# Feed-forward of a decoder layer: order of the inner and down parts, the last inner tile, and the closing sums

## What is computed

```python
gate = x2 @ Wg          # 512 -> 1376
up = x2 @ Wu            # 512 -> 1376
inter = gate * jax.nn.sigmoid(gate) * up
out = (inter @ Wd).astype(jnp.float16)   # 1376 -> 512
```

## Time and profile before

| | us |
|---|---|
| median of 3 runs | 779.55 (778.93 to 779.99) |
| the profiled execution, its time | 780.11 |
| its span in the trace | 777.8 |
| first matmul of window 0 | 632.25 |
| first matmul of window 10 | 741.63 |
| first matmul of the down parts of tile 10 | 761.90 |

### The profile page before, as it was taken

How to read it: one execution, slowest core, us unless ns; L and a number is a source line. 1 busy time by engine, 2 the same in 40 slices (tenths; PEclk the granted TensorE clock), 3 DMA queues, 4 the chain that set the end, 5 groups by cost and what they waited for, 6 DMA issues and landing times.

```text
span 777.8 us, 11268 instructions
## 1 busy us (share of the span) xinstructions
PE 749.0 (96%) x3764; PEld 623.4 (80%) x3764; DVE 504.4 (65%) x664; ACT 383.3 (49%) x964; POOL 308.3 (40%) x333
## 2 busy tenths in 40 slices
PE   7999999999999999999999999999999869999994
PEld 6888888888888888888888888888887647777763
...
GB/s 298 110 56 78 14 91 108 77 69 35 155 30 104 47 128 0 94 108 57 48 37 135 30 65 24 111 0 262 22 1 2 1 0 78 59 81 35 28 10 108
DMA packets 43807, 54.34 MB, mean 70 GB/s; under 512 B 7400, under 2 KB 26024, under 8 KB 43784
## 3 DMA queue, kind: packets, MB, share of 16 engines
...
## 4 chain that ended last, share of the span: by engine, by line
PE 89%; DVE 4%; POOL 2%; issue 2%; ACT 2%; DMA 1%; SPq 0%; DVEq 0%; POOLq 0%; ACTq 0%
PE psum L425 20%; PE psum L427 20%; PE psum L426 20%; PE psum L552 7%; PE psum L626 6%; PE psum L627 5%; PE psum L561 3%; PE psum L634 3%; PE psum L635 2%; PE psum L431 1%; DVE stats L1032 1%; PE psum L445 1%; DMA xacc<-in_x 1%; PE psum L530 1%; DVE xacc L1265 1%
## 5 line engine op out<-in xcount | busy, mean ns | idle before, releaser
L954 POOL TENSOR_TENSOR probs<-probs,rowinv 128x512 f32<-128x512 f32 x64 | 71.1, 1111 | 308.7 <-DVE rowinv L1177 308.7
L785 ACT ACTIVATE probs<-probs,negmax 128x128 f32<-128x128 f32 x256 | 99.8, 391 | 60.4 <-DVE negmax L1164 60.4
L425 PE MATMUL psum<-xt_hi,wq_hi 128*128 128x512 f32 x256 | 104.4, 408 | 0.0
L425 PE MATMUL psum<-wo_hi,at_hi 128*128 128x512 f32 x256 | 100.2, 391 | 0.5 <-DVE at_lo L1195 0.5
L427 PE MATMUL psum<-xt_hi,wq_lo 128*128 128x512 f32 x256 | 100.2, 391 | 0.0
L426 PE MATMUL psum<-xt_lo,wq_hi 128*128 128x512 f32 x256 | 99.9, 390 | 0.0
L427 PE MATMUL psum<-wo_hi,at_lo 128*128 128x512 f32 x256 | 99.7, 389 | 0.0
L426 PE MATMUL psum<-wo_lo,at_hi 128*128 128x512 f32 x256 | 99.6, 389 | 0.0
L778 ACT CAST pt_hi<-psum 128x512 fp32r<-128x512 f32 x64 | 37.5, 587 | 124.6 <-PE psum L561 124.6
L1195 DVE TENSOR_TENSOR at_lo<-psum,at_hi 128x512 fp32r<-128x512 f32 x64 | 44.1, 689 | 72.7 <-ACT at_hi L814 72.7
L689 ACT ACTIVATE qt<-psum 128x512 f32<-128x512 f32 x64 | 38.0, 594 | 75.7 <-PE psum L427 74.1
(11 more groups left out here) (128 smaller groups left out, 1647.0 us busy)
## 6 DMA issues: line engine op xcount, KB each, us to landing
...
```

The lines of the kernel that those rows point to most:

```text
L425: pe.matmul(dst, a_hi, b_hi, start=start, stop=False)
L785: e = act.activation(probs[:, t % 2, j, :], probs[:, t % 2, j, :], ACT.Exp, bias=negmax[:, t % 2, j:j + 1], accum_out=rowsum[:, t % 2, j:j ...
L954: pool.tensor_tensor(probs[:, t % 2], probs[:, t % 2], rowinv[:, t % 2, :].unsqueeze(2).to_broadcast([P, HG, P]), ALU.mult).then_inc(prob_ ...
```

## The change

Four edits. **Order:** in windows 2 to 10 the down parts stand between the gate and up parts: positions 0 to 3 gate and up, 4 down 0, 5 and 6 gate and up, 7 down 2, 8 and 9 gate and up, 10 down 1, 11 down 3. ACT takes positions 0, 1, 4 and 7, DVE the others; on ACT both down parts now stand ahead of Silu, and on POOL the sum of down part 0 ahead of the inner product. **Last inner tile:** the product and int_lo of tile 10 are made by DVE. **Closing sums:** DVE does all four chunks of token half 0 and chunks 2 and 3 of half 1; ACT and POOL do chunks 0 and 1 of half 1. ACT and POOL add output blocks 1, 3 and 6, over y_part. **Tail of the attention:** the first token halves of the first four gate and up parts of window 0 are computed in slots 10 to 13, one in each, into even banks.

```diff
+        GU_AT = (0, 1, 2, 3, 5, 6, 8, 9)
+        D_AT = (4, 10, 7, 11)
+        ACT_AT = (0, 1, 4, 7)
+        LAST_WINDOW = NT + LAG - 2
+
+        def gu_at(n, k):
+            return GU_AT[k] if n >= LAG else k
+
+        def d_at(c, j):
+            return D_AT[j] if c + LAG < NT else j
+
+        def length(n):
+            return GU * (n < NT) + HC * (n >= LAG)
...
+        def by_act(n, k):
+            return k in (ACT_AT if LAG <= n < NT else (0, 1) if n < LAG else (0, 2))
...
+            return (n, k - HC) if k >= HC else (n - 1, k - HC + length(n - 1))
...
-        LAST_ACT = 1
-        LAST_DVE = [j for j in range(HC) if j != LAST_ACT]
+        LAST_TURNS = [(0, 0), (0, 1), (0, 3), (0, 2), (1, 2), (1, 3)]
+        LAST_POOL = (0, 1)
+        Y_POOL = (1, 3, 6)
...
-                sp.wait_ge(y_ready, b + 1)
+                if b in Y_POOL:
+                    sp.wait_ge(y_pool, Y_POOL.index(b) + 1)
+                else:
+                    sp.wait_ge(y_dve, b + 1 - sum(i < b for i in Y_POOL))
...
-            for t in range(SLOTS, ALL_SLOTS):
-                cross_scores(t)
-                turn_queries(t)
-                cross_output(t)
-                turn_third(t)
...
-            def gate_up(n):
+            def gate_up_half(n, c, m, k, h):
...
+                cols = slice(h * HALF, (h + 1) * HALF)
+                dst = psum[0:w, 2 * (k % HC) + h, :]
+                pe.matmul(dst, gw[:, r, m, c, 0:w], ft_hi[:, c, cols], start=True, stop=False)
+                return pe.matmul(dst, gw[:, r, m, c, 0:w], ft_lo[:, c, cols], start=False, stop=True)
+
+            def gate_up(n, c, m):
+                k = gu_at(n, 2 * c + m)
+                if c == 0 and m == 0:
+                    pe.wait_ge(ld_gu[n % RING_GU], (n // RING_GU + 1) * TILE_LOADS)
+                part_free(n, k)
+                for h in range(1 if (n, k) < (0, HC) else 0, NH):
+                    mm = gate_up_half(n, c, m, k, h)
+                mm.then_inc(part_done, 1)
...
-            def down(c):
-                pe.wait_ge(ld_d[c % RING_D], (c // RING_D + 1) * 16)
-                pe.wait_ge(intlo_ready, c + 1)
-                for j in range(HC):
-                    part_free(c + LAG, GU + j)
-                    for h in range(NH):
-                        mm = down_half(c, j, h, 2 * j + h)
-                    mm.then_inc(part_done, 1)
-
...
+            def down(c, j):
+                k = d_at(c, j)
+                if j == 0:
+                    pe.wait_ge(ld_d[c % RING_D], (c // RING_D + 1) * 16)
+                    pe.wait_ge(intlo_ready, c + 1)
+                part_free(c + LAG, k)
+                for h in range(NH):
+                    mm = down_half(c, j, h, 2 * (k % HC) + h)
+                mm.then_inc(part_done, 1)
+
+            for t in range(SLOTS, ALL_SLOTS):
+                cross_scores(t)
+                k = t - SLOTS
+                if k == 0:
+                    pe.wait_ge(ln_lo[2], BH)
+                    pe.wait_ge(o_added, ATT + PRIME)
+                    pe.wait_ge(ld_gu[0], TILE_LOADS)
+                gate_up_half(0, k // 2, k % 2, k, 0)
+                turn_queries(t)
+                cross_output(t)
+                turn_third(t)
             pe.wait_ge(ln_lo[2], NB)
-            pe.wait_ge(o_added, ATT + PRIME)
-            for n in range(NT + LAG - 1):
-                if n < NT:
-                    gate_up(n)
-                if n >= LAG:
-                    down(n - LAG)
+            for n in range(LAG):
+                for c in range(HC):
+                    gate_up(n, c, 0)
+                    gate_up(n, c, 1)
+            for n in range(LAG, NT):
+                gate_up(n, 0, 0)
+                gate_up(n, 0, 1)
+                gate_up(n, 1, 0)
+                gate_up(n, 1, 1)
+                down(n - LAG, 0)
+                gate_up(n, 2, 0)
+                gate_up(n, 2, 1)
+                down(n - LAG, 2)
+                gate_up(n, 3, 0)
+                gate_up(n, 3, 1)
+                down(n - LAG, 1)
+                down(n - LAG, 3)
+            for j in range(HC):
+                down(NT - LAG, j)
 
...
             for b in range(NB):
-                h = b // BH
-                pe.wait_ge(last_dve, (h + 1) * len(LAST_DVE))
-                pe.wait_ge(last_pool, h + 1)
+                if b < BH:
+                    pe.wait_ge(last_dve, HC)
+                else:
+                    pe.wait_ge(last_dve, len(LAST_TURNS))
+                    pe.wait_ge(last_pool, len(LAST_POOL))
...
@@ -870,18 +906,20 @@
                     inner_first(n - 1)
                 if n >= LAG:
                     down_part(n - LAG, 0)
+                if n >= LAG:
+                    down_part(n - LAG, 2)
                 if n < NT:
                     w = width(n)
-                    done, count = copied(n, GU - 2)
+                    done, count = copied(n, gu_at(n, GU - 2))
                     act.wait_ge(done, count)
                     act.activation(f_g[0:w, n % 2], f_g[0:w, n % 2], ACT.Silu).then_inc(silu_ready, 1)
-                if n >= LAG:
-                    down_part(n - LAG, 2)
-            for h in range(NH):
-                act.wait_ge(last_done, h * HC + LAST_ACT + 1)
-                act.wait_ge(o_summed, 2 * (NT - 2) - 1 + h)
-                act.mul(o_part[:, h, 0:HALF], psum[:, h * HC + LAST_ACT, :],
-                        d_s[:, LAST_ACT, NT - 1:NT]).then_inc(last_part, 1)
+            for i, j in enumerate(LAST_POOL):
+                act.wait_ge(last_done, HC + j + 1)
+                act.wait_ge(o_summed, 2 * (NT - 2) - 1 + i)
+                act.mul(o_part[:, i, 0:HALF], psum[:, HC + j, :], d_s[:, j, NT - 1:NT]).then_inc(last_part, 1)
+            for i, b in enumerate(Y_POOL):
+                act.wait_ge(y_turned, b + 1)
+                act.copy(y_part[:, i], psum[:, b, :].bitcast(F16)[:, 0:H]).then_inc(y_copied, 1)
...
 
             for n in range(NT + LAG - 1):
-                if n < NT:
+                if n >= LAG + 1:
+                    down_sum(n - LAG, 0)
+                if n < NT - 1:
                     inner(n)
-                for j in (0, 2):
-                    if n >= LAG + 1:
-                        down_sum(n - LAG, j)
-                if n < NT:
+                if n >= LAG + 1:
+                    down_sum(n - LAG, 2)
+                if n < NT - 1:
                     inner_second(n)
-            for h in range(NH):
-                cols = slice(h * HALF, (h + 1) * HALF)
-                pool.wait_ge(last_part, h + 1)
-                done, count = copied(NT + LAG - 2, GU + LAST_ACT)
-                pool.wait_ge(done, count)
-                pool.tensor_tensor(o16[:, LAST_ACT, cols], o_part[:, h, 0:HALF], o_sum[:, LAST_ACT, cols],
+            for i, j in enumerate(LAST_POOL):
+                pool.wait_ge(last_part, i + 1)
+                if j % 2:
+                    done, count = copied(LAST_WINDOW, j)
+                    pool.wait_ge(done, count)
+                else:
+                    pool.wait_ge(o_summed, 2 * (NT - 2) - 1 + j // 2)
+                pool.tensor_tensor(o16[:, j, HALF:T], o_part[:, i, 0:HALF], o_sum[:, j, HALF:T],
                                    ALU.add).then_inc(last_pool, 1)
+            for i, b in enumerate(Y_POOL):
+                pool.wait_ge(y_copied, i + 1)
+                pool.tensor_tensor(xacc[:, b, :], y_part[:, i], xacc[:, b, :], ALU.add).then_inc(y_pool, 1)
...
-            for n in range(NT + LAG - 1):
-                if n < NT:
-                    for k in range(2, GU):
-                        part_add(n, k)
+            for n in range(NT):
+                for c in range(1, HC):
+                    part_add(n, c, 0)
+                    part_add(n, c, 1)
+                if n == NT - 1:
+                    w = width(n)
+                    done, count = copied(n, gu_at(n, GU - 1))
+                    dve.wait_ge(done, count)
+                    dve.wait_ge(silu_ready, NT)
+                    dve.tensor_tensor(f_u[0:w, n % 2], f_g[0:w, n % 2], f_u[0:w, n % 2], ALU.mult).then_inc(int_ready, 1)
                 if n >= LAG:
-                    for j in (1, 3):
-                        down_add(n - LAG, j)
-
-            for h in range(NH):
+                    down_add(n - LAG, 1)
+                    down_add(n - LAG, 3)
+            n, w = NT - 1, width(NT - 1)
+            dve.wait_ge(inthi_ready, NT)
+            dve.wait_ge(intlo_ready, NT - 1)
+            dve.tensor_tensor(int_lo[0:w, n % RING_I], f_u[0:w, n % 2], int_hi[0:w, n % RING_I].bitcast(F32),
+                              ALU.subtract).then_inc(intlo_ready, 1)
+            down_add(NT - LAG, 1)
+            down_add(NT - LAG, 3)
+
+            for h, j in LAST_TURNS:
                 cols = slice(h * HALF, (h + 1) * HALF)
-                for j in LAST_DVE:
-                    dve.wait_ge(last_done, h * HC + j + 1)
-                    if j % 2:
```

(21 more changed lines are left out.)

67 lines of the change are left out of this document (25 added, 42 removed).

## The result

The changed kernel takes 771.94 us (769.68 to 772.6, 4 runs) where the kernel before takes 779.77 beside it: a ratio of 0.9895 with a 95% interval of 0.9871 to 0.9918. Forecast was 771.6. The profiled execution has a span of 770.7 and a time of 772.6, at a mean clock of 0.990.

What follows compares the result with a forecast made beforehand. PE, busy 96% of the span, was taken as the bound, so only its waits could shrink. Terms 2.4 + 0.9 + 1.9 + 2.7 = 7.9 took the median from 779.55 to 771.6, range 767.8 to 774.6.

Steps and rivals of the forecast that it cites:

- Start, 2.40: Ahead of window 0: hidden half parts let DVE's sixth part end its wait at 641.42 instead of 643.82, gain 2.40.
- the sum: The prediction's part-by-part reckoning over the whole kernel: 2.4 + 0.9 + 1.9 + 2.7 = 7.9 us off the span.
- the rival on the clock: Low clock from 628 on begins later or is shorter, DVE's first part 0.6 to 1.8 earlier: 770.2, chance 0.18.
- Window 2: Window 2: the new order spreads DVE's parts and no slot is late, 8.36 instead of 9.28, gain 0.92.
- windows 3 to 9: Seven windows: PE's slot wait of 0.27 each goes, period 11.0 instead of 11.28, gain 1.9.
- End, 2.7: From window 10's start to the span's end: about 33.5 instead of 36.2, gain 2.7.
- makes the last 16 matmuls from there, at 2.4 GHz: End: after PE's stand from 16.6 to 18.8, the last 16 matmuls take some 4.0 instead of 6.7.
- The rival: Clock falls in PE's 2.2 us stand at the end; 14 slow matmuls cost 2.8, partly beside DVE: 773.6, chance 0.08.
- The lock: End: POOL's sums hold up DVE's product and int_lo, near 2.1 and 3.1 long; without it 3.0 shorter.
- no lock: Rival: DVE's product and int_lo run beside POOL, int_lo ends 2.7 to 3.0 earlier: 768.7, chance 0.12.

Runs made afterwards that it cites:

- e8: Changed kernel plus 28 matmuls of no use in PE's gaps of slots 10 to 13 and ahead of window 0; 769.65 us, ratio 0.9886 to the kernel before.
- e10: Changed kernel with int_lo of the last tile ahead of DVE's down part (8, 3), plus 28 filler matmuls at the start; 768.31 us, ratio 0.9860.
- e3: Changed kernel with the four down parts of a window back behind the eight gate and up parts, on all engines; 773.77 us, ratio 0.9917.
- e6: Changed kernel plus eight matmuls of no use in PE's gap ahead of the last 16 matmuls; 770.77 us, ratio 0.9885 to the kernel before.
- e1: The changed kernel unaltered, timed again beside the kernel before, on the chip of e2 to e4; 771.25 us, ratio 0.9881.
- e7: Changed kernel with all eight output blocks added by DVE, none by ACT and POOL; 772.14 us, ratio 0.9900 to the kernel before.
- e11: The changed kernel unaltered, run once more on the same chip as e9 and e10; 772.36 us, ratio 0.9912 to the kernel before.
- e2: Changed kernel without the four half parts ahead of window 0; 773.91 us, ratio 0.9920 to the kernel before.
- e9: Changed kernel with one DVE instruction moved: int_lo of the last tile ahead of down part (8, 3); 769.14 us, ratio 0.9883 to the kernel before.
- e4: Changed kernel with the last tile's product and int_lo made by POOL again; 773.39 us, ratio 0.9899 to the kernel before.
- e12: Same kernel as e4, run once more unaltered; 770.12 us, ratio 0.9887 to the kernel before.
- e5: Changed kernel with POOL's last three sums cut to one column each, work left out; 767.80 us, ratio 0.9850 to the kernel before.

## Why the prediction was right, and where it was off

**Start, 2.40; it measured 2.85.** Mechanism right: the four half parts lie in gaps, DVE's first part was to move to 635.28 and its sixth to 641.42, and they stand at 634.99 and 640.96. The 0.46 beyond is the clock. The last transposes ahead of window 0, before and in the changed kernel:

```profile
629.73 1.12 PE L431 MATMUL psum<-ident,xm 128*128 128x128 f32 x4 [1.92 <-ACT xm L706]
```

```profile
629.90 0.66 PE L443 MATMUL psum<-ident,xm 128*128 128x128 f32 x4 [1.45 <-ACT xm L741]
```

They took 0.66 instead of 1.12, and with that window 0 starts 0.29 earlier. The six matmuls that DVE's first part then waits for were slow, as forecast. The rest comes from the matmuls behind 635.4, which are at 2.4 GHz, where before they were slow until 638.4: the fifth part is ready sooner than the 637.84 of the sum, and DVE starts it at 637.38. That is the first half of the rival on the clock, in part. By e8 and e10, 632.5 is what the start gives with no low stretch.

**Window 2 and windows 3 to 9, 0.92 and 1.9.** The period is 10.99 (11.0 forecast), so seven windows gave 2.0 and window 2 the other 0.84 of the 2.87 measured; e3, with the old order, gives back 2.89. No slot was late. DVE's pair of down parts took 2.47, less than the 2.65 used; in e3 it takes 2.65 again, so this goes with the order. Why is not shown.

**End, 2.7: this is the term that was mis-sized; it measured 1.40.** From window 10's start (735.91) the steps up to PE's return held: product issued at 11.1 (10.92 forecast) and over at 13.0 (12.97); int_lo over at 18.6 (18.7); PE idle 2.07 (2.2), back at 18.7 (18.8). The next step failed: "makes the last 16 matmuls from there, at 2.4 GHz". They ran at 1.2 GHz. DVE, which was to hold the end, waits 1.15 for PE, and from there all is 1.3 late: DVE's last half chunk at 26.6 (25.25), first store at 27.2 (25.95), end at 34.8 (33.5). e6, which fills the gap, ends at 33.63, so the clock accounts for 1.16 of the 1.3.

The rival had this with a chance of 0.08 and a price of 2.0, for the reason that 2.2 of idle time is less than the 3.07 and 5.11 behind which the clock had been seen low. That reading of the trace before left out its longest low stretch, the one from 628.1 to 638.4:

```profile
623.67 1.12 PE L530 MATMUL psum<-cx,xprobs 128*128 128x512 f32 x2 [1.58 <-DVE xprobs L1100]
...
627.19 0.63 PE L431 MATMUL psum<-ident,xm 128*128 128x128 f32 x4 [1.96 <-DVE ft_lo L1038]
```

The matmuls at 627.19 were still fast and those at 629.73 (above) slow, and no gap around them is over 1.96. So gaps of under 2.2 had been followed by the low clock already, where several stood close together. In the changed kernel, too, a slot wait of 1.08 stands shortly ahead of the 2.07 (750.15; the sum itself had it, at 14.3): PE was idle 3.15 of the 5.55 us before 754.62. No sure rule comes of that. Of six profiles with both gaps, four were low for all 16 matmuls (the changed kernel's, e1, e7, e11), e8 for 8, and e2 not at all. e3, with one gap of 2.10, was low for the 8 matmuls ahead of the last 16. e6, e9 and e10, without a gap of 2, were not low.

**The tile's move.** The sum followed int_lo on DVE and never worked out the same end with the tile left on POOL. By e4 and e12 PE comes back at 18.3 then, 0.4 sooner. Before, it came back at 20.27. So with the new order this edit took 0.4 away from PE instead of giving, and the 1.56 that PE gained against before is the order's; with the old order (e3, 19.02) the tile on DVE does go with an earlier return, by 1.25.

**The lock.** Forecast 2.1 and 3.1 for the two DVE instructions, measured 1.90 and 3.31; "no lock" is refuted by e5 and e9 together. The prediction named the GPSIMD Engine Reference of the Trainium skill. Another page of the Trainium skill, SBUF — State Buffer, section "SBUF: two separate sides", says more: the instruction that starts first holds the shared ports for all of its length and the other is blocked. By that rule the trace agrees in both directions, with 1.22 against 3.31 on DVE and 2.37 against 3.35 on POOL.

**The sum.** 2.85 + 2.87 + 1.40 = 7.12 in the profiled executions; between the medians it is 7.83. The low stretches of the clock differ from one execution to the next (in the three profiles of the changed kernel DVE's first part lies between 633.80 and 634.99), so the closeness of 771.94 to 771.6 is in part luck: start 0.45 better and end 1.3 worse than forecast.
